# Moving Wo's products, the gate, the output transposes, the norm's sums and lane 0's old-state products between slots of a hand-ordered loop

## What is computed

```
q, k, v = short convolution (4 taps) and silu of x @ Wq, x @ Wk, x @ Wv     (k and v three times per token)
per token:  S = S * exp(g);  three times  S = S + beta * k (v - k S);  o = q S
gate = x @ Wg
o = o * rsqrt(mean(o*o) + 1e-5) * rms_weight * silu(gate)
y = o.reshape(heads * 128) @ Wo
x1 = layernorm(x + y)
out = layernorm(x1 + ffn(x1))
```

## Time and profile before

| | |
|---|---|
| median of 3 runs | 8102.13 us (8089.04 to 8104.49) |
| profiled execution | 8104.79 us, span 8103.0 us |
| mean granted TensorE clock | 0.960 of full |
| TensorE busy | 7272.4 us (90%), loading weights 6184.4 us (76%) |
| VectorE busy | 6431.8 us (79%) |
| ScalarE busy | 5452.1 us (67%) |
| GpSimd busy | 4114.1 us (51%) |
| DMA | mean 12 GB/s |

### The profile page before, as it was taken

One profiled execution on the slowest core, in us unless ns is written; L12 is line 12 of the kernel. 1 busy time (PEld: TensorE's weight loads), 2 busy tenths in 40 slices (PEclk: granted clock), 3 DMA queues, 4 the chain that ended last, 5 costly groups with the idle time before them and its releaser, 6 DMA issues. The chain is left out here.

```text
span 8103.0 us, 425307 instructions
## 1 busy us (share of the span) xinstructions
PE 7272.4 (90%) x155940; PEld 6184.4 (76%) x155940; DVE 6431.8 (79%) x22300; ACT 5452.1 (67%) x20343; POOL 4114.1 (51%) x6333
## 2 busy tenths in 40 slices
PE   5899999989989898989898889898988989889999
PEld 3777777777777777777777777777777777767777
DVE  4888888888888888888888888888888888533333
ACT  3777777777777777777777777777777777433333
POOL 0555555555556555555555555555555555411111
PEclk6899999999999999999999999999999999899999
DMA  2000000000000000000000000000000000000000
GB/s 91 8 9 9 10 9 10 9 10 9 10 9 10 10 10 10 9 10 9 10 9 10 10 9 10 10 10 9 10 10 9 10 10 10 19 19 8 10 8 8
DMA packets 283508, 96.47 MB, mean 12 GB/s; under 512 B 226097, under 2 KB 276545, under 8 KB 281153
## 3 DMA queue, kind: packets, MB, share of 16 engines
q1 hardware_dynamic: 281408, 68.93, 3.9%
HBM read 52.08 MB, written 16.78 MB: 8 GB/s over the span
## 5 line engine op out<-in xcount | busy, mean ns | idle before, releaser
L823 DVE SCALAR_TENSOR_TENSOR CY<-PP,CWV,CY 128x128 f32<-128x128 f32 x4608 | 1588.2, 345 | 103.8 <-ACT CY L740 13.7
L823 DVE SCALAR_TENSOR_TENSOR CY<-PP,CWK,CY 128x128 f32<-128x128 f32 x4608 | 1584.0, 344 | 74.8 <-ACT CY L740 0.7
L1035 POOL TENSOR_TENSOR UM<-U,C 32x256 f32<-32x256 f32 x1536 | 1105.0, 719 | 119.6 <-POOL UM L1035 26.5
L1028 POOL TENSOR_TENSOR Y<-U,C 32x256 f32<-32x256 f32 x768 | 553.6, 721 | 1017.8 <-DVE UQ L916 977.7
L532 PE MATMUL PP<-XT,WV 128*128 128x131 f32 x3072 | 736.6, 323 | 259.0 <-DVE CY L823 226.2
L532 PE MATMUL PP<-XT,WK 128*128 128x131 f32 x3072 | 739.0, 323 | 253.8 <-DVE CY L823 253.7
L1008 POOL TENSOR_TENSOR S<-R,BETA 96x4 f32<-96x4 f32 x512 | 101.3, 198 | 1401.6 <-DVE R L876 1310.8
L740 ACT ACTIVATE CY<-PP,CWK 128x128 f32<-128x128 f32 x1536 | 565.4, 368 | 351.3 <-PE PP L532 339.0
L1241 ACT ACTIVATE HS<-PH,B1S 128x512 f32<-128x512 f32 x512 | 351.7, 687 | 608.1 <-PE PH L1160 608.1
L532 PEld LDWEIGHTS PP<-XT,WV 128*128 128x128 f32 x3072 | 476.8, 196 | 364.4 <-DVE CY L823 299.5
L812 ACT ACTIVATE KQ<-CY 128x128 f32<-128x128 f32 x2048 | 740.6, 362 | 7.8
(11 more groups left out here) (228 smaller groups left out, 18959.3 us busy)
## 6 DMA issues: line engine op xcount, KB each, us to landing
EX<-exd SPq DMA_DIRECT2D x768, 32.0 KB, 2.2
exd<-EXS SPq DMA_DIRECT2D x16, 512.0 KB, 2.7
XR<-in_L_attn_x SPq DMA_DIRECT2D x65, 64.0 KB, 1.9
XL<-in_L_attn_x SPq DMA_DIRECT2D x16, 256.0 KB, 2.9
XRES<-in_L_attn_x SPq DMA_DIRECT2D x64, 64.0 KB, 2.6
x<-X SPq DMA_DIRECT2D x64, 64.0 KB, 2.9
XI<-x SPq DMA_DIRECT2D x16, 256.0 KB, 2.9
out<-OUT SPq DMA_DIRECT2D x16, 256.0 KB, 2.3
```

The lines of the kernel that those rows point to most:

```text
L823: dve.scalar_tensor_tensor(CY[:, m % RING], ptile(m)[:, s:s + P], taps_of(m)[:, s:s + 1], CY[:, m % RING], ALU.mult, ALU.add).then_inc(tap ...
L1028: pool.tensor_tensor(Y1[r, :, :], U[r, par, :, r], over(first[r, :], [BK, NHEAD, BK], 1), ALU.mult).then_inc(seed_sb, 1)
L1035: pool.tensor_tensor(UM[r, lv], U[r, par, :, r], over(merge[lv][r, :], [BK, NHEAD, BK], 1), ALU.mult).then_inc(made, 1)
```

## The change

Five kinds of steps change their slot; none is added or taken away, and what each computes and waits for stays.

- TensorE: the products with the old state of lane 0 in slot 0 in place of 1, in every chunk.
- Output transposes (chunk 2) and gate products (chunk 3), two groups each: slots 9 and 10 in place of 8 and 10, with ScalarE's copies.
- Wo's products (chunk 2): slot 13 in place of 12.
- YL: slot 0 of chunk 3 in place of slot 13 of chunk 2, second part in both; bn_stats and bn_aggr in slot 1 in place of 0, the addition in slot 2 in place of 1.
- FA: slot 3, second part, in place of slot 2, first part.

```diff
--- before.py
+++ after.py
...
                             invert(invn, 1 - par, INV_AT[k])
                         if known(i, 0, NSC):
                             project(i, half, SLOTS * c + k)
-                        if k in (1, 4) and do_run:
+                        if k in (0, 4) and do_run:
                             old_state(k // 4, run, rs, rc)
                         if do_inv and k == 4:
                             invert(invn, 1 - par, INV_AT[k])
...
                             new_state(k - 10, run, rc, prep, do_prep)
                         if k in (12, 13) and do_prep:
                             rows_v(k - 12, c, sc, prep, run, do_run)
-                        if k in (8, 10) and out_now:
-                            l = (k - 8) // 2
+                        if k in (9, 10) and out_now:
+                            l = k - 9
                             if l == 0:
                                 need(pe, join_sb, 3 * run + 3 if do_run else 0)
                                 if not do_run:
...
                             for h in range(LH):
                                 mm = pe.transpose(quad[:, h], OG[:, 2 * l + h // 2, h % 2], ident)
                             mm.then_inc(ogt_ps, 1)
-                        if k in (8, 10) and gate_now:
-                            l = (k - 8) // 2
+                        if k in (9, 10) and gate_now:
+                            l = k - 9
                             if l == 0:
                                 if do_run:
                                     pe.wait_ge(join_sb, 3 * run + 3)
...
                                 for j in range(LH):
                                     mm = pe.matmul(quad[CT * j:CT * j + CT, 2 * cc:2 * cc + 2], XT[:, 1 - half, t0:t0 + CT], wg[:, :, j], start=True, stop=True)
                             mm.then_inc(gate_ps, 1)
-                        if k == 12 and out_now:
+                        if k == 13 and out_now:
                             pe.wait_ge(ogt_sb, 2 * (i - 1))
                             for h in range(NHEAD):
                                 mm = pe.matmul(PB[:, 0:P], OGT[:, h], WO[:, h], start=(h == 0), stop=(h == NHEAD - 1))
...
                             if rc == 0:
                                 need(act, og_sb, 2 * (i - 1))
                             act.activation(OSB[:, rc], PA[:, 0:2], ACT.Copy).then_inc(o_sb, 1)
-                        if k in (8, 10) and out_now:
-                            q, l = i - 2, (k - 8) // 2
+                        if k in (9, 10) and out_now:
+                            q, l = i - 2, k - 9
                             act.wait_ge(ogt_ps, 2 * q + l + 1)
                             act.wait_ge(sso_sb, 2 * q + 2)
                             to = OGT[:, :, 2 * CT * l:2 * CT * l + 2 * CT].rearrange("p h (c t) -> p c h t", c=2)
                             act.activation(to, PB[:, :].rearrange("p (c h t) -> p c h t", c=2, h=NHEAD), ACT.Copy).then_inc(ogt_sb, 1)
-                        if k in (8, 10) and gate_now:
-                            q, l = i - 1, (k - 8) // 2
+                        if k in (9, 10) and gate_now:
+                            q, l = i - 1, k - 9
                             act.wait_ge(gate_ps, 2 * q + l + 1)
                             need(act, og_sb, 2 * q)
                             act.activation(GSIL[:, 2 * l:2 * l + 2], PB[:, :].rearrange("p (c g d) -> p c g d", c=2, g=2), ACT.Silu).then_inc(gsil_sb, 1)
...
                             op = dve.scalar_tensor_tensor(BZ[:, h], PA[:, h % LH], HEADD[:, run, h:h + 1], VP[:, par, h], ALU.mult, ALU.add)
                         if part == 1:
                             op.then_inc(b_sb, 1)
-                    if k == 2 and out_now and part == 0:
+                    if k == 3 and out_now and part == 1:
                         q = i - 2
                         dve.wait_ge(sso_sb, 2 * q + 2)
                         dve.wait_ge(qse_sb, q + 1)
...
                             dve.tensor_tensor(UQ[0:R, c, lanes[l]], PK[0:R, lanes[l], R:P], EM[0:R, lanes[l], R:P], ALU.mult).then_inc(u_sb, 1)
                     if k == 11 and do_run:
                         add_state(0, run, part, 2)
-                    if k == 13 and out_now and part == 1:
+                    if k == 0 and norm_now and part == 1:
                         q = i - 2
                         dve.wait_ge(wo_ps, q + 1)
                         dve.wait_ge(xres_in[half], 8 * (q + 2 - half) if not isinstance(q, int) else 16 * ((q + 2) // 2))
                         dve.tensor_tensor(YL[:, :], PB[:, 0:P], XRES[:, half], ALU.add).then_inc(y_sb, 1)
-                    if k == 0 and norm_now and part == 0:
+                    if k == 1 and norm_now and part == 0:
                         dve.wait_ge(y_sb, i - 1)
                         dve.bn_stats(ST[:, :], YL[:, :]).then_inc(st_sb, 1)
-                    if k == 0 and norm_now and part == 1:
+                    if k == 1 and norm_now and part == 1:
                         dve.wait_ge(st_sb, i - 1)
                         dve.memset(spare[:, :], 0.0)
                         dve.bn_aggr(MV[:, :], ST[:, :]).then_inc(mv_sb, 1)
-                    if k == 1 and norm_now and part == 0:
+                    if k == 2 and norm_now and part == 0:
                         dve.wait_ge(mv_sb, 2 * (i - 2) + 1)
                         dve.tensor_scalar(MV[:, 1:2], MV[:, 1:2], EPS_LN, None, ALU.add).then_inc(mv_sb, 1)
                     if k == 4 and norm_now and part == 1:
```

## The result

The changed kernel takes **8193.0 us** (median of 4 runs, 8170.4 to 8226.5) beside 8103.3 us (8089.0 to 8112.0) for the kernel before: ratio **1.011, 95% interval 1.008 to 1.015**. It is some 90 us slower, where 137 us less were forecast; it lies outside the range.

A forecast was written before the change was run, and what follows sets the result against it. Neither TensorE nor VectorE is saturated; stretches bounded by each alternate, coupled by three PSUM banks. Terms of 56, 66, 14 and 3 us make 139 off 8104.8 or 8102.1: forecast 7965 us, range 7890 to 8046.

The forecast's parts named there:

- I count nothing: TensorE's clock falls in slots 6 to 13 of chunks 2 or 3: no gain or loss put into the sum.
- rival (c): Less idle time keeps TensorE's clock up: 83 us more gained, 7882; turned round, some 50 lost, 8015; chance 0.10.
- About 1 us of idle ahead of slot 7 stays; the one of slot 4 goes: TensorE's idle time in chunk 2: about 1 us ahead of slot 7 remains, the 1.40 ahead of slot 4's projection disappears.
- FA, 0.9: Norm's sums moved to slot 3 of chunk 2: wait and operations leave slot 2, 0.9 us per block gained.
- the margin of 0.5: GpSimd's queue in chunk 2: KDS, behind FB, still ready 0.5 us before ScalarE's KD can start; nothing lost, bounds 0 to 0.5.
- Wo, 1.06: Wo's products moved in chunk 2: TensorE's idle times in slots 1 and 4 of chunk 3 go, 1.06 us per block gained.
- near 20: Sign of being right: VectorE's wait ahead of slot 13's Y in chunk 2 falls from 122.8 us to near 20.
- Old state, 0.3 in chunk 0: Lane 0's old-state products moved to slot 0: 0.3 us gained in chunk 0, in 48 blocks; nothing in chunks 1 and 2.
- Gate and transposes, 0.05 gained: Output transposes and gate moved to slots 9 and 10: chunk 3 gains 0.05 us, chunk 2 nothing.
- (a): Half a gain: idle freed by Wo's move returns in slot 7 of chunk 3, KDS holds ScalarE; 8046 us, chance 0.13.
- (b): Slower: slot 1's projection, pushed behind the old state, sets slot 2's tap; 90 us more, 8192, chance 0.04.
- (d): No effect: TensorE at 90% is the bound, each removed idle time made up by another; within 0.2%, chance 0.05.

The follow-up runs named there:

- the kernel with the idle time filled: The changed kernel with slot 6's projection issued 3, 1, 7 and 4 times more in chunks 0 to 3: 7926.6 us, ratio 0.979.
- the filled kernels: Kernel before and changed kernel, each with slot 6's projection repeated (3, 1, 4, 4 and 3, 1, 7, 4 times more): 8058.4 and 7926.6 us.

## Why the prediction was wrong

**The clock, "I count nothing".** This is the term that failed. The prediction saw the falls in the very parts concerned (they hold 4.0 of the 6.1 us of low time before; 2.1 lie in chunks 0 and 1, which it didn't read), and took it that less idle time would leave them or lessen them; turned round, rival (c) was given "some 50" of loss and called "in the forecast's range". The prediction's own sign for a wrong clock, a mean that moves by over 0.01 from 0.960, came: 0.934. The low time rose by 7.4 us per block. What it costs: the mean block lies 2.91 above the clean one before and 6.64 after, 3.73 more for 7.4 us of low time, 0.50 for each us; with the clean block's 2.22 less that is 1.51 per block, 94 us in 62 blocks, and 90 were measured. Against the kernel with the idle time filled, 10.4 us less of low time are 4.17 us of block, 0.40 for each us. A straight line through the 58 blocks of one kernel gives 0.37 before and 0.40 after. So the price is 0.4 to 0.5; at 0.4 the low time explains 3.0 of the 3.73, and the rest stays open.

**"About 1 us of idle ahead of slot 7 stays; the one of slot 4 goes".** The second half came true in the main, the first did not. TensorE of the kernel before, the projection of slot 7 in block 30, chunk 2, and then of the kernel after, those of slots 4 and 7:

```profile
3366.54 0.81 PE L532 MATMUL PP<-XT,WK 128*128 128x131 f32 x2 [0.94 <-DVE CY L823]
```

```profile
3398.70 0.49 PE L532 MATMUL PP<-XT,WK 128*128 128x131 f32 x2 [0.39 <-DVE CY L823]
...
3404.45 0.49 PE L532 MATMUL PP<-XT,WK 128*128 128x131 f32 x2 [1.35 <-DVE CY L823]
```

TensorE reaches slot 7 the earlier for what it no longer waits in slot 4 (1.40 before, 0.39 after in block 30), and there it waits for the taps of slot 5, which come earlier by less. Summed by place over blocks 8 to 59, its idle time fell from 10.8 to 9.3 us per block. Ahead of slot 4's projection in chunk 2 it fell from 1.45 to 0.37; ahead of slot 7's it rose from 0.87 to 1.34, and behind that slot's Gram products from 0.52 to 1.04, together from 1.39 to 2.38. The idle time was less in sum and gathered around slot 7. FA's move alone took chunk 2's low time in slots 6 to 13 from 2.5 to 4.4. That the falls hang on this idle time is shown for the kernel after by the fills, of all chunks and of chunk 2 alone; that FA's move alone acts through it is argued from the place.

**FA, 0.9 (bounds 0.5 to 1.1).** Measured 1.09 in the clean block, at the upper bound. ScalarE did hold slot 5's first tap as argued. VectorE of the kernel after, chunk 2:

```profile
3400.07 0.17 DVE L897 TENSOR_SCALAR FA<-QSE 128x8 f32<-128x8 f32 x1
...
3402.27 0.35 DVE L823 SCALAR_TENSOR_TENSOR CY<-PP,CWK,CY 128x128 f32<-128x128 f32 x1 [0.17 <-ACT CY L740]
```

There is no wait ahead of FA. KD waited for KDS once, 0.2 us: the margin of 0.5 on GpSimd's queue held, and nothing was lost there.

**Wo, 1.06 (0.4 to 1.8).** Measured 1.35. Y's wait went from 122.8 to 6.8, further than the "near 20" named; YL waits for Wo 6.9 in two cases, in none of the loop's blocks. TensorE's idle time ahead of the projections of slots 1 and 4 of chunk 3 went from 0.64 and 0.44 to 0.00, as worked out from the earlier trace rows. This is 1.08 of the 1.35; with Wo's move alone the clean block gains 1.38. Where the other 0.3 comes from was not traced.

**Old state, 0.3 in chunk 0.** Measured 0.30: the shortest chunk 0 is 23.81 and, with this part undone, 24.11; the others differ by 0.01 at most, 0.33 over the block. The blocks where the loop starts anew were not looked at by themselves.

**Gate and transposes, 0.05 gained (0 to 0.3).** Measured 0.54 lost, wrong in sign. "TensorE has no idle time from slot 7 to 10" was read in chunk 3, and "the same place: nothing" was said for chunk 2 without reading it. In chunk 2 there was an idle time in slot 8 that took the transposes in, and the new place lies ahead of an inverse step. Of the loss 0.44 is there and 0.13 in chunk 3. The bounds left out a loss with no reason that excludes one.

These four make 2.23 gained (1.09 + 1.35 + 0.33 - 0.54) for a forecast of 2.2: two terms low by 0.5 together, one wrong by 0.6. The sum was right by luck of the signs, and the time of the filled kernels, 132 us apart, agrees.

**The rivals.** (a), half a gain, fell: KDS held nothing, and ahead of slot 7 of chunk 3 only 0.18 of idle time came back (1.00 to 1.18). (b) named 8192, almost the measured time, and is wrong all the same: no chunk is longer in the clean block through slot 1's projection, and chunk 0 is shorter. (c) had the right quantity, the low clock; its good end, 7882, is about what the filled kernels reach (7927 and 7866). Its bad end was put at 50 us and is 180 to 230 (62 times 7.4 us of low time at 0.4 to 0.5). (d) fell with the clean block.

**What stays open.** That low clock time took the gain, that the idle time around slot 7 brings most of it, and that the two stretches influence each other is shown by the fills, of all stretches and of one. Why the two large moves together give 13.4 or more where alone they give 8.8 and 4.4 is not; they weren't tried without either of the small ones. Content of a stretch alone, a shift in chunk 0 and the spacing of the two stretches alone fell as causes. Work put between the two stretches takes 4 to 5 us of the low time, but does not bring it to the 6.1 of before, and isn't separated from what it fills.

## What to carry to other kernels

Take a schedule's gain and the clock's price apart before a change is judged: the shortest time of each stretch over all passes of the loop shows the one, the granted clock of the stretches the other. Here they were -2.2 and +3.7 us per block, and a change that removes waits was slower, because the idle time left to TensorE lay more around one place and the clock fell there more often. The shortest time is only clean where some passes have no fall in that stretch; count them. Where an idle time can't be removed, repeating a product that is there anyway, into the same bank and ahead of the one that signals, can be worth more than the edit it is put beside (8193 to 7927 us here); five products per block more brought no further gain (7866 to 7892).

## What was not expected of the hardware

- Less idle time on TensorE (10.8 to 9.3 us per block) went with more time at the lower clock (6.1 to 13.5 us).
- The clock fell behind idle times as short as 1.37 and 1.17 us with 1.03 us of Gram products between them, and in another block it did not behind 1.35 and 0.53.
- Falls of stretches 27 us apart are coupled: seven products in chunk 2 took 3.0 us of low time from chunk 3 (4.87 to 1.83); four in chunk 3 took 4.3 from there, and 5.2 more came up in chunks 0 and 1.
- Low time cost 0.4 to 0.5 us of block for each us at the lower level (0.37 and 0.40 from block to block within the kernels before and after, 0.50 between their means).
